# Last stage of a graph network kernel: edge slots summed into windows of 128 nodes that step by 64, in place of node tiles

## The chip, the cores and the metric

The kernel runs on one core of a Trainium2 chip. The metric is the device time of one execution in microseconds. The kernel before took 3025.7 us (median of 3 runs, 3021.4 to 3028.46).

## The reference, cut to what is computed

Four blocks follow each other, each added to x (6250 nodes of 256 features): a graph convolution over 100000 edges, a mixture of 8 experts, a second graph convolution, and a second mixture of 32 experts of which each node takes the one with the highest score. The change touches the second convolution and what follows it:

```python
h = layernorm(x) @ weight                                  # L1_gnn
msgs = edge_weight[:, None] * h[src]
x = x + segment_sum(msgs, dst, 6250) + bias
xf = layernorm(x)                                          # L1_ffn
idx = argmax(xf @ router_w.T + router_b)
x = x + relu(relu(xf @ W1[idx] + b1[idx]) @ W2[idx] + b2[idx])
```

The edges come sorted by `dst`, the node that an edge adds to. Both ends are drawn uniformly, so that 16 edges on average go to each node and 2048 to a tile of 128 nodes.

## The kernel before, in words

Nodes are held in 49 tiles of 128 rows. The edges are padded to 784 columns of 128 edges, and four columns (512 edges, 32 nodes on average) make a slot: 196 slots. Four programs run one after the other. The first converts the edge lists, checks them and computes the first products; the second does the first convolution and the 8 experts; a general path for edge lists that don't fit (`edge_block`) is skipped when the check of the first program finds nothing; the last stage, from line 1836, does the second convolution and the 32 experts.

In the last stage a loop over slots s is written out in full on each engine, with semaphores between them:

- GpSimd (POOL) issues four indirect DMAs per slot (line 2024). Each fetches 128 rows of 2 KB of `h_tab[1]`, one for each edge, into a ring of four slots (`got`). Slot s waits until the products of slot s - 4 are done (`s_prod`).
- VectorE (DVE) makes in its slot s the one-hot matrices of slot s + 1 (`one_hot`, line 2227): for each of the four columns a high and a low table, in which row e has the weight of edge e in the column of its node. There are two buffers, so that it waits for the products of slot s - 1.
- TensorE (PE) multiplies them with the fetched rows (`edges`, lines 2125 to 2127), three matmuls per column and node tile (high by high, high by low, low by high), and sums in one of two banks, `tile_bank(t)`. Slots 1 and 2 of a tile's four (s % 4) reach one node tile. Slots 0 and 3 lie at an edge of a tile and reach two, with a table 256 wide and 24 matmuls in place of 12. I call these wide and the others narrow slots.
- When a tile's last slot is done, DVE adds the bank to the tile's rows (line 2261), and takes the layer norm's statistics. Over the next six slots the tile is normalised, transposed and routed to its expert (lines 2188, 2197, 2203 on PE; 2267 to 2307 on DVE).
- The expert layers run from slot 11 on, for groups of four tiles: one step of the 16 per group in each slot. A step is 7 matmuls of 512 columns (`hidden`, lines 2142 to 2146), a ReLU on ScalarE (ACT, line 2076), its low half on DVE (line 2254), and 12 matmuls of 256 columns (`outputs`, lines 2163 to 2167) two slots later. After the 196th slot 26 more remain, with expert work alone.
- SyncE (SP) loads a group's rows from `acc_tab` (line 2045) after the rows of three groups before have been stored (line 2060), since they share the place.

The order of the work in a slot on PE is `edges(s)`, `outputs`, `hidden`, then a tile's small steps. On DVE it is the four additions of a finished group (line 2245), `one_hot(s + 1)`, the low half, then the tile's steps. In the first program `outside()` counts the edges that lie outside the reach of their slot's tiles (lines 743 to 756).

Of the kernel before, what the change touches and what calls it, by code (L numbers as in the profile page):

```python
# [61 lines left out]
FARS = 7  # L62
# [18 lines left out]
def build(nc, x, src, dst, wgt, wl, wr, bl, br, gw, gbr, w1, b1, g1, be1, m1, v1,  # L81
          w2, b2, g2, be2, m2, v2, wo, bo, lw, lb, rw, rb, mw1, mb1r, mw2, mb2, out):
    ctx = ExitStack()
    with ctx:
# [138 lines left out]
        with ExitStack() as c1:  # L223
# [53 lines left out]
            with ExitStack() as cc, nc.Block() as block:  # L277
# [58 lines left out]
                def _(pool):  # L336
# [35 lines left out]
                                   base=0, channel_multiplier=0).then_inc(s_const, 1)  # L372
                    nc.gpsimd.memset(ones[:, :], 1.0).then_inc(s_const, 1)
# [270 lines left out]
                def _(dve):  # L644
                    dve.wait_ge(s_const, 11)
# [9 lines left out]
                    nc.vector.tensor_copy(rel_n[:, :], node_i[:, :]).then_inc(s_bsum, 1)  # L655
# [85 lines left out]
                    def outside():  # L741
# [4 lines left out]
                        nc.vector.tensor_scalar(same[:, :], rel_n[:, :], float(2 * P), None, ALU.is_ge).then_inc(s_far, 1)  # L746
# [3 lines left out]
                        dve.wait_ge(s_far, 3)  # L750

                        def between(a):
                            return a[:, :].rearrange("p (t j) -> p t j", t=NTILES)[:, :, REACH:-REACH]
# [1082 lines left out]
        with ExitStack() as c4, nc.Block() as block:  # L1836
# [91 lines left out]
            hot_h = sb4("n1_hot_h", [P, 2, U, 2 * P], F32R)  # L1928
            hot_l = sb4("n1_hot_l", [P, 2, U, 2 * P], F32R)
# [46 lines left out]
            def node_tiles(s):  # L1976

                t, r = divmod(s, U)
                pairs = ((t - 1, 0), (t, P)) if r == 0 else ((t, 0), (t + 1, P)) if r == U - 1 else ((t, 0),)
                return [(q, at) for q, at in pairs if 0 <= q < NTILES]  # L1980

            def tile_bank(t):
                return bank[6 + t % 2][:, 0:D]
# [21 lines left out]
            def _(pool):  # L2005
                nc.gpsimd.iota(iota_i[:, :], pattern=[[1, 2 * P]], base=0, channel_multiplier=0).then_inc(s_node, 1)

                first = node_i[:, :].rearrange("p (t j) -> p t j", t=NTILES)
                nc.gpsimd.iota(first[:, :, 0:REACH], pattern=[[P, NTILES], [0, REACH]], base=-P,
                               channel_multiplier=0).then_inc(s_node, 1)  # L2010
                nc.gpsimd.iota(first[:, :, REACH:], pattern=[[P, NTILES], [0, EDGE_TILES // NTILES - REACH]],
                               base=0, channel_multiplier=0).then_inc(s_node, 1)
# [51 lines left out]
            def _(act):  # L2064
                act.wait_ge(s_keep, 1)
                act.wait_ge(s_node, 5)
# [43 lines left out]
            def _(pe):  # L2110
                def edges(s):
                    for t, at in node_tiles(s):

                        if t >= 2 and s == t * U - 1:
                            pe.wait_ge(s_sum, t - 1)

                    pe.wait_ge(s_got[s % RING], (s // RING + 1) * (16 * U))
                    pe.wait_ge(s_hot, s + 1)
                    for u in range(U):
                        for t, at in node_tiles(s):  # L2120
                            begins = u == 0 and s == max(t * U - 1, 0)
                            ends = u == U - 1 and s + 1 == edges_end(t)
                            w_h, w_l = hot_h[:, s % 2, u, at:at + P], hot_l[:, s % 2, u, at:at + P]
                            m_h, m_l = (got[:, s % RING, u, a:a + D] for a in (0, D))
                            nc.tensor.matmul(tile_bank(t), w_h, m_h, start=begins, stop=False)  # L2125
                            nc.tensor.matmul(tile_bank(t), w_h, m_l, start=False, stop=False)  # L2126
                            last = nc.tensor.matmul(tile_bank(t), w_l, m_h, start=False, stop=ends)  # L2127
                    last.then_inc(s_prod, 1)
# [77 lines left out]
            def _(dve):  # L2206
                nc.vector.tensor_copy(gidx, src_f[:, :]).then_inc(s_gidx, 1)
                nc.vector.tensor_scalar(wgt_f[:, :], wgt_f[:, :], keep[:, 0:1], None, ALU.mult).then_inc(s_keep, 1)
                dve.wait_ge(s_node, 3)
                nc.vector.tensor_copy(iota_f[:, :], iota_i[:, :]).then_inc(s_node, 1)  # L2210
                nc.vector.tensor_tensor(rel_n[:, :], dst_f[:, :], node_i[:, :], ALU.subtract).then_inc(s_node, 1)
                dve.wait_ge(s_node, 5)
# [6 lines left out]
                def one_hot(s):  # L2219

                    n = 2 * P if s % U in (0, U - 1) else P
                    if s >= 2:
                        dve.wait_ge(s_prod, s - 1)
                    for weight, table in ((dst_f, hot_h), (wgt_f, hot_l)):
                        for u in range(U):
                            c = s * U + u
                            last = nc.vector.tensor_scalar(table[:, s % 2, u, 0:n], iota_f[:, 0:n], rel_n[:, c:c + 1],  # L2227
                                                           weight[:, c:c + 1], ALU.is_equal, ALU.mult)
# [9 lines left out]
                for s in range(SLOTS):  # L2238
# [145 lines left out]
```

## Time and profile before

| | |
|---|---|
| Median of 3 runs | 3025.7 us (3021.4 to 3028.46) |
| Span of the profiled execution | 3226.6 us |
| Instructions in the profile | 53400 |
| Last stage in the profile | 1891 to 3226 us, 1335 us |

The profile is of one execution, which was slower than the timed runs by 200.9 us. Nothing in it says where these went. Engines are named PE (matmul), PEld (its weight load), DVE, ACT, POOL and SP; a matmul's duration is modelled and overlaps the next one, so that the distance between two starts tells more than the duration. PEclk is the clock that was granted to TensorE as a share of 2.4 GHz. In the view by lines a group shows its count, its busy time and the mean of one, then the idle time of the engine before them and what ended it. "issue" is time for which the profile shows no cause.

### The profile page before, as it was taken

Reading aid. Unit: us, or ns where it says so; the run is one execution under the profiler, and the core shown is the slowest. Engines: PE = TensorE matmul, PEld = TensorE weight load, DVE = VectorE, ACT = ScalarE, POOL = GpSimd, SP = SyncE. Lnnn points to the kernel's source line nnn. Section 1 sums busy time; section 2 is a strip of 40 time slices with the busy share of each in tenths; the row PEclk is TensorE's granted clock in tenths of the full one; section 3 lists DMA queues with packets and bytes.
Section 4 is the critical chain, followed back from the end, with each engine's and each line's share of the span. In section 5 each row is a group of like instructions: output and inputs, shape, how many; then the busy total and the mean of one; then the engine's idle time right before and its main releaser. Section 6 shows DMA issues by size and latency. Waiting matters only on the chain. (4 is left out here: it accounts for less than half of the span.)

```text
span 3226.6 us, 53400 instructions
## 1 busy us (share of the span) xinstructions
PE 2795.6 (87%) x18900; PEld 2527.3 (78%) x18900; DVE 2177.2 (67%) x5025; ACT 1527.1 (47%) x3161; POOL 1939.5 (60%) x1692
## 2 busy tenths in 40 slices
PE   5899737899999999999999936799999998999999
PEld 5798626788888788888888736788888888888888
DVE  8889654667777777777776555566666666666653
ACT  4477456878888788888876510011111111111111
POOL 0455477677677677777772047666666666666640
PEclk9999856899999999999999977899999999999999
DMA  2143452223323332333231057767777676766650
GB/s 68 7 91 76 106 173 88 77 89 105 95 88 107 102 101 81 107 105 101 81 104 52 20 173 188 180 170 180 179 185 180 167 182 174 179 171 176 177 138 14
DMA packets 241570, 390.22 MB, mean 121 GB/s; under 512 B 43258, under 2 KB 114834, under 8 KB 241042
## 3 DMA queue, kind: packets, MB, share of 16 engines
q0 software_dynamic: 163072, 310.24, 37.3%
q1 hardware_dynamic: 77940, 74.90, 7.3%
q8 instruction: 153, 2.51, 0.3%
q10 hardware_dynamic: 288, 1.61, 0.1%
q14 instruction: 117, 0.96, 0.1%
HBM read 343.43 MB, written 43.19 MB: 120 GB/s over the span
## 5 line engine op out<-in xcount | busy, mean ns | idle before, releaser
L1328 POOL DMA_INDIRECT f_got<-h_tab,list_cols x784 | 964.5, 1230 | 348.9 <-issue 237.9
L2024 POOL DMA_INDIRECT n_got<-h_tab,edge_cols x784 | 802.2, 1023 | 429.6 <-issue 219.0
L2076 ACT ACTIVATE n_hrh<-bank 128x512 fp32r<-128x512 f32 (+1 forms) x208 | 119.3, 573 | 1080.7 <-remote 644.6
L1623 DVE TENSOR_TENSOR f_hlo<-edge_cols,f_hhi 128x1024 fp32r<-128x1024 f32 (+1 forms) x208 | 242.3, 1165 | 310.0 <-ACT f_hhi L1418 229.4
L1507 PE MATMUL bank<-f_mhi,f_hot 128*128 128x256 f32 x1168 | 326.2, 310 | 108.7 <-DVE f_mlo L1617 101.7
L2125 PE MATMUL bank<-n_got,n_hot_h 128*128 128x256 f32 x1168 | 355.0, 304 | 74.3 <-issue 47.5
L1388 ACT ACTIVATE f_got<-f_got,list_cols 128x256 f32<-128x256 f32 x784 | 333.7, 497 | 110.3 <-DMA f_got<-h_tab,list_cols 106.3
L1413 ACT ACTIVATE edge_cols<-bank,f_shf,f_scl 128x512 f32<-128x512 f32 (+1 forms) x416 | 296.4, 745 | 186.9 <-PE bank L1319 120.2
L2127 PE MATMUL bank<-n_got,n_hot_l 128*128 128x256 f32 x1168 | 341.6, 292 | 12.0 <-issue 11.5
L2126 PE MATMUL bank<-n_got,n_hot_h 128*128 128x256 f32 x1168 | 341.6, 293 | 9.9 <-issue 9.6
L2227 DVE TENSOR_SCALAR n_hot_h<-list_cols,rel_f,edge_cols 128x256 fp32r<-128x256 f32 (+1 forms) x784 | 250.5, 387 | 138.6 <-DMA acc<-acc_tab 93.4
L2254 DVE SCALAR_TENSOR_TENSOR n_hrl<-bank,n_hrh 128x512 fp32r<-128x512 f32 (+1 forms) x208 | 136.5, 656 | 306.0 <-ACT n_hrh L2076 209.5
L1507 PEld LDWEIGHTS bank<-f_mhi,f_hot 128*128 128x128 f32 x1168 | 244.3, 209 | 124.1 <-issue 118.7
L1508 PE MATMUL bank<-f_mlo,f_hot 128*128 128x256 f32 x1168 | 316.1, 302 | 0.4 <-issue 0.4
L2125 PEld LDWEIGHTS bank<-n_got,n_hot_h 128*128 128x128 f32 x1168 | 234.0, 200 | 88.8 <-issue 61.2
L380 POOL DMA_INDIRECT list<-runs,off_i x98 | 162.9, 1663 | 216.7 <-DVE off_i L739 101.8
L1617 DVE TENSOR_TENSOR f_mlo<-f_got,f_mhi 128x1024 fp32r<-128x1024 f32 x196 | 239.2, 1220 | 18.4 <-issue 12.3
L1508 PEld LDWEIGHTS bank<-f_mlo,f_hot 128*128 128x128 f32 x1168 | 245.4, 210 | 5.0 <-issue 0.9
L2227 DVE TENSOR_SCALAR n_hot_l<-list_cols,rel_f,edge_cols 128x256 fp32r<-128x256 f32 (+1 forms) x784 | 248.0, 395 | 0.0
L2126 PEld LDWEIGHTS bank<-n_got,n_hot_h 128*128 128x128 f32 x1168 | 234.5, 201 | 15.9 <-issue 14.1
L2127 PEld LDWEIGHTS bank<-n_got,n_hot_l 128*128 128x128 f32 x1168 | 234.0, 200 | 13.6 <-issue 13.4
L2165 PE MATMUL bank<-n_w2l,n_hrh 128*128 128x256 f32 x784 | 226.4, 289 | 15.0 <-issue 14.9
(332 smaller groups left out, 7462.7 us busy)
## 6 DMA issues: line engine op xcount, KB each, us to landing
f_got<-h_tab,list_cols POOLq DMA_INDIRECT x784
n_got<-h_tab,edge_cols POOLq DMA_INDIRECT x784
h_tab<-acc SPq DMA_DIRECT2D x37, 128.0 KB
edge_cols<-in_w SPq DMA_DIRECT2D x16, 256.0 KB
xn<-acc_tab SPq DMA_DIRECT2D x8, 512.0 KB
n_rows<-acc_tab SPq DMA_DIRECT2D x8, 512.0 KB
out_rows<-n_rows SPq DMA_DIRECT2D x8, 512.0 KB
acc<-in_x SPq DMA_DIRECT2D x4, 896.0 KB
```

What stands on the lines that cost most here:

```text
L1328: nc.gpsimd.indirect_dma_start(got[:, s % RING0, u, :], None, h_tab[0], bass.IndirectOffsetOnAxis(gidx0[:, s * U + u:s * U + u + 1], 0), b ...
L1388: last = nc.scalar.activation(got[:, s % RING0, u, :], got[:, s % RING0, u, :], ACT.Copy, scale=w0_f[:, c:c + 1])
L1413: nc.scalar.activation(rl[:, m, 0:w], bank[(i + m) % 3][:, 0:w], ACT.Relu, bias=shf[:, l, e, m:m + 1], scale=scl[:, l, e, m:m + 1]).then_i ...
L1507: nc.tensor.matmul(tile_bank(t), lhs, mhi[:, s % 2, u, :], start=begins, stop=False)
L1508: last = nc.tensor.matmul(tile_bank(t), lhs, mlo[:, s % 2, u, :], start=False, stop=ends)
L1617: nc.vector.tensor_tensor(mlo[:, s % 2, :, :], got[:, s % RING0, :, :], mhi[:, s % 2, :, :].bitcast(F32), ALU.subtract).then_inc(s_mlo, 1)
L1623: nc.vector.tensor_tensor(hlo[l][:, :, 0:w], rl[:, :, 0:w], hhi[l][:, :, 0:w].bitcast(F32), ALU.subtract).then_inc(s_lo[l], 1)
L2024: nc.gpsimd.indirect_dma_start(got[:, s % RING, u, :], None, h_tab[1], bass.IndirectOffsetOnAxis(gidx[:, s * U + u:s * U + u + 1], 0), bou ...
L2125: nc.tensor.matmul(tile_bank(t), w_h, m_h, start=begins, stop=False)
L2126: nc.tensor.matmul(tile_bank(t), w_h, m_l, start=False, stop=False)
L2127: last = nc.tensor.matmul(tile_bank(t), w_l, m_h, start=False, stop=ends)
L2227: last = nc.vector.tensor_scalar(table[:, s % 2, u, 0:n], iota_f[:, 0:n], rel_n[:, c:c + 1], weight[:, c:c + 1], ALU.is_equal, ALU.mult)
```

## The change

In place of node tiles, slots 2m - 1 and 2m are summed in one window m of 128 nodes, which begins at node 64 (m - 1). There are 99 windows. Each slot has tables 128 wide and 12 matmuls. A window lies in one bank, m % 2. It covers one node tile when m is odd, and the upper half of one tile and the lower half of the next when m is even, so that DVE adds it with one or two instructions (`window_parts`): 147 additions in place of 49. DVE adds window m in slot 2m + 1. The first half tile of tile t is added in slot 4t + 1, where before the tile was first touched in slot 4t + 5; the statistics stay in slot 4t + 5. In the first program the check of the edge lists follows the windows: three more iotas on POOL, two fewer instructions on DVE.

```diff
+WIN_TILES = 2 * U
+WINDOWS = (EDGE_TILES - 2 * U) // WIN_TILES + 2
+HALF_NODES = P // 2
...
+        def window_bases(cols, landed):
+            body = cols[:, U:EDGE_TILES - U].rearrange("p (m j) -> p m j", j=WIN_TILES)
+            nc.gpsimd.iota(cols[:, 0:U], pattern=[[0, U]], base=-HALF_NODES, channel_multiplier=0).then_inc(landed, 1)
+            nc.gpsimd.iota(body, pattern=[[HALF_NODES, WINDOWS - 2], [0, WIN_TILES]], base=0,
+                           channel_multiplier=0).then_inc(landed, 1)
+            nc.gpsimd.iota(cols[:, EDGE_TILES - U:], pattern=[[0, U]], base=(WINDOWS - 2) * HALF_NODES,
+                           channel_multiplier=0).then_inc(landed, 1)
...
+                    window_bases(rel_n[:, :].bitcast(I32), s_const)
...
-                    dve.wait_ge(s_const, 11)
+                    dve.wait_ge(s_const, 14)
...
-                        nc.vector.tensor_scalar(same[:, :], rel_n[:, :], float(2 * P), None, ALU.is_ge).then_inc(s_far, 1)
+                        nc.vector.tensor_scalar(same[:, :], rel_n[:, :], float(P), None, ALU.is_ge).then_inc(s_far, 1)
...
-                        nc.vector.tensor_scalar(between(same), between(rel_n), float(P), None, ALU.is_ge).then_inc(s_far, 1)
-                        dve.wait_ge(s_far, 4)
-                        nc.vector.tensor_reduce(far_n[:, 2:3], between(same), AX.XY, ALU.add).then_inc(s_far, 1)
...
+            def window_of(s):
+                return (s + 1) // 2
+            def window_bank(m):
+                return bank[6 + m % 2][:, 0:D]
+            def window_parts(m):
+                t, odd = divmod(m, 2)
+                parts = ((t, 0, P),) if odd else ((t - 1, HALF_NODES, P), (t, 0, HALF_NODES))
+                return [(q, a, b) for q, a, b in parts if 0 <= q < NTILES]
...
                 def edges(s):
-                    for t, at in node_tiles(s):
-                        if t >= 2 and s == t * U - 1:
-                            pe.wait_ge(s_sum, t - 1)
+                    m = window_of(s)
+                    opens, closes = s == 0 or s % 2 == 1, s % 2 == 0 or s == EGROUPS - 1
+                    if opens and m >= 2:
+                        pe.wait_ge(s_sum, m - 1)
...
                     for u in range(U):
-                        for t, at in node_tiles(s):
...
+                        w_h, w_l = hot_h[:, s % 2, u, :], hot_l[:, s % 2, u, :]
+                        nc.tensor.matmul(window_bank(m), w_h, m_h, start=(opens and u == 0), stop=False)
+                        nc.tensor.matmul(window_bank(m), w_h, m_l, start=False, stop=False)
+                        last = nc.tensor.matmul(window_bank(m), w_l, m_h, start=False, stop=(closes and u == U - 1))
...
                 def one_hot(s):
-                    n = 2 * P if s % U in (0, U - 1) else P
+                    at = P // 2 if window_of(s) % 2 == 0 else 0
...
+                    if s % 2 == 1 and s <= EGROUPS + 1:
+                        m = (s - 1) // 2
+                        dve.wait_ge(s_prod, min(s, EGROUPS))
+                        if m:
+                            dve.wait_ge(s_sum, m)
+                        for q, a, b in window_parts(m):
+                            dve.wait_ge(s_accin, group_of(q) * 16 + 16)
+                            last = nc.vector.tensor_tensor(row(q)[a:b, :], window_bank(m)[a:b, :], row(q)[a:b, :], ALU.add)
+                        last.then_inc(s_sum, 1)
                     t = tile_at(s, AT_SUM)
                     if t is not None:
-                        dve.wait_ge(s_prod, edges_end(t))
-                        dve.wait_ge(s_accin, group_of(t) * 16 + 16)
-                        nc.vector.tensor_tensor(row(t), tile_bank(t), row(t), ALU.add).then_inc(s_sum, 1)
-                        dve.wait_ge(s_sum, t + 1)
+                        dve.wait_ge(s_sum, 2 * t + 3)
                         nc.vector.bn_stats(stats[:, t % 2, :], row(t)).then_inc(s_stats, 1)
```

## Rows read from the trace of the kernel before

**Rows 1.** The page: busy times, and the granted clock in 40 slices.
```profile
PE 2795.6 (87%) x18900; PEld 2527.3 (78%) x18900; DVE 2177.2 (67%) x5025; ACT 1527.1 (47%) x3161; POOL 1939.5 (60%) x1692
PEclk9999856899999999999999977899999999999999
```
**Rows 2.** Windows: length, busy PE, PEld, DVE, ACT, POOL (instructions), clock, DMA share, GB/s.
```profile
1891.00:3226.00 1335.00, 1172.06 (x7753) 1064.19 (x7753) 814.71 (x2681) 169.03 (x411) 806.77 (x789) 0.94 0.65 168
...
1967.00:2100.00 133.00, 101.80 (x616) 94.74 (x616) 72.10 (x264) 11.07 (x39) 88.05 (x88) 0.78 0.70 179
2100.00:3100.00 1000.00, 915.77 (x6163) 828.77 (x6162) 633.07 (x2122) 126.34 (x314) 639.96 (x633) 0.97 0.69 176
3145.00:3220.00 75.00, 75.00 (x477) 67.22 (x475) 22.80 (x52) 15.85 (x31) 0.00 (x0) 1.00 0.02 8
```
**Rows 3.** Line 2024, the gathers: duration ns min/median/max, first and last start.
```profile
L2024 POOL DMA_INDIRECT n_got<-h_tab,edge_cols x784: 997/1003/3233, 1893.5 to 3126.4; - x196
```
**Rows 4.** Timeline of POOL: start, duration, what [idle before, releaser].
```profile
2419.22 1.00 POOL L2024 DMA_INDIRECT n_got<-h_tab,edge_cols  x1 [0.30 <-issue]
2422.47 1.13 POOL L2024 DMA_INDIRECT n_got<-h_tab,edge_cols  x1 [2.25 <-PE bank L2127]
```
**Rows 5.** Timeline of PE: first edge matmuls of slots, and a stall.
```profile
2408.93 0.36 PE L2125 MATMUL bank<-n_got,n_hot_h 128*128 128x256 f32 x1
...
2415.27 0.36 PE L2125 MATMUL bank<-n_got,n_hot_h 128*128 128x256 f32 x1
2415.47 0.28 PE L2126 MATMUL bank<-n_got,n_hot_h 128*128 128x256 f32 x1
2415.59 0.28 PE L2127 MATMUL bank<-n_got,n_hot_l 128*128 128x256 f32 x1
...
2419.80 0.28 PE L2125 MATMUL bank<-n_got,n_hot_h 128*128 128x256 f32 x1
...
2421.59 0.28 PE L2125 MATMUL bank<-n_got,n_hot_h 128*128 128x256 f32 x1 [0.91 <-issue]
...
2425.37 0.36 PE L2125 MATMUL bank<-n_got,n_hot_h 128*128 128x256 f32 x1
...
2431.48 0.36 PE L2125 MATMUL bank<-n_got,n_hot_h 128*128 128x256 f32 x1
```
**Rows 6.** Timeline of DVE: a narrow and a wide pair of tables, a tile's addition.
```profile
2440.12 1.12 DVE L2227 TENSOR_SCALAR n_hot_h<-list_cols,rel_f,edge_cols 128x128 fp32r<-128x128 f32 x4 [1.40 <-DMA acc<-acc_tab]
2441.15 1.11 DVE L2227 TENSOR_SCALAR n_hot_l<-list_cols,rel_f,edge_cols 128x128 fp32r<-128x128 f32 x4
2443.11 0.41 DVE L2261 TENSOR_TENSOR xn<-bank,xn 128x256 f32<-128x256 f32 x1
2443.56 0.43 DVE L2263 BATCH_NORM_STATS2 n_stats<-xn 128x6 f32<-128x256 f32 x1
2445.63 1.38 DVE L2227 TENSOR_SCALAR n_hot_h<-list_cols,rel_f,edge_cols 128x256 fp32r<-128x256 f32 x4
2446.92 1.38 DVE L2227 TENSOR_SCALAR n_hot_l<-list_cols,rel_f,edge_cols 128x256 fp32r<-128x256 f32 x4
```
**Rows 7.** Line 1699: a DVE instruction that reads a bank on 8 partitions.
```profile
L1699 DVE TENSOR_TENSOR f_gateT<-bank,f_gateT x13: 280/680/681, 511.6 to 1794.0; 8x512 fp32r<-8x512 f32 x12, 8x128 fp32r<-8x128 f32 x1
```
**Rows 8.** Timeline of SP and DVE: a group's store, its load, the first addition.
```profile
2389.25 0.38 SPq L2060 DMA_DIRECT2D out_rows<-n_rows  x1
2394.22 0.37 SPq L2045 DMA_DIRECT2D n_rows<-acc_tab  x1
...
2467.85 0.41 DVE L2261 TENSOR_TENSOR n_rows<-bank,n_rows 128x256 f32<-128x256 f32 x1
```
**Rows 9.** Timeline of the first program: an iota, DVE's wait, the check's last instruction.
```profile
4.93 0.77 POOL L371 IOTA node_i<- 128x588 int32 x1
13.11 0.63 DVE L667 CAST xnt<-base 112x896 f32<-112x896 int32 x1 [4.57 <-DMA hbuf<-in_wgt]
...
128.26 0.56 DVE L756 TENSOR_REDUCE far_n<-rel_f 128x1 f32<-128x392 f32 x1
```

More of the change, by code:

```diff
@@ L61 @@
 SCANS = 7
-FARS = 7
+FARS = 5
+WIN_TILES = 2 * U
+WINDOWS = (EDGE_TILES - 2 * U) // WIN_TILES + 2
+HALF_NODES = P // 2
 EARLY = 3
@@ L654, in _ @@
                     nc.vector.memset(lag[:, :], 0.0)
-                    nc.vector.tensor_copy(rel_n[:, :], node_i[:, :]).then_inc(s_bsum, 1)
+                    nc.vector.tensor_copy(rel_n[:, :], rel_n[:, :].bitcast(I32)).then_inc(s_bsum, 1)
                     dve.wait_ge(s_bsum, 1)
@@ L749, in outside @@
                                                        accum_out=far_n[:, 1:2]).then_inc(s_far, 1)
-                        dve.wait_ge(s_far, 3)
-                        def between(a):
-                            return a[:, :].rearrange("p (t j) -> p t j", t=NTILES)[:, :, REACH:-REACH]
-                        nc.vector.tensor_scalar(between(same), between(rel_n), float(P), None, ALU.is_ge).then_inc(s_far, 1)
-                        dve.wait_ge(s_far, 4)
-                        nc.vector.tensor_reduce(far_n[:, 2:3], between(same), AX.XY, ALU.add).then_inc(s_far, 1)
                     def scales(g):
@@ L1927, in build @@
             got = sb4("n1_got", [P, RING, U, 2 * D], F32R)
-            hot_h = sb4("n1_hot_h", [P, 2, U, 2 * P], F32R)
-            hot_l = sb4("n1_hot_l", [P, 2, U, 2 * P], F32R)
+            hot_h = sb4("n1_hot_h", [P, 2, U, P], F32R)
+            hot_l = sb4("n1_hot_l", [P, 2, U, P], F32R)
             wgt_h = dst_f.bitcast(F32R)
@@ L1974, in width @@
                 return WIDTHS[g]
[L1976 to L1983, printed above, removed]
+            def window_of(s):
[6 more added lines that the diff above has]
+                return [(q, a, b) for q, a, b in parts if 0 <= q < NTILES]
             def out_tile(k):
@@ L2005, in _ @@
             def _(pool):
[L2006 to L2012, printed above, removed]
+                nc.gpsimd.iota(iota_i[:, :], pattern=[[0, 2], [1, P]], base=0, channel_multiplier=0).then_inc(s_node, 1)
+                window_bases(node_i[:, :], s_node)
                 pool.wait_ge(s_gidx, 1)
@@ L2065, in _ @@
                 act.wait_ge(s_keep, 1)
-                act.wait_ge(s_node, 5)
+                act.wait_ge(s_node, 6)
                 nc.scalar.activation(wgt_h[:, :], wgt_f[:, :], ACT.Copy).then_inc(s_wgt, 1)
@@ L2119, in edges @@
                     for u in range(U):
-                        for t, at in node_tiles(s):
[L2121 to L2127, printed above, removed]
+                        w_h, w_l = hot_h[:, s % 2, u, :], hot_l[:, s % 2, u, :]
+                        m_h, m_l = (got[:, s % RING, u, a:a + D] for a in (0, D))
+                        nc.tensor.matmul(window_bank(m), w_h, m_h, start=(opens and u == 0), stop=False)
+                        nc.tensor.matmul(window_bank(m), w_h, m_l, start=False, stop=False)
+                        last = nc.tensor.matmul(window_bank(m), w_l, m_h, start=False, stop=(closes and u == U - 1))
                     last.then_inc(s_prod, 1)
@@ L2208, in _ @@
                 nc.vector.tensor_scalar(wgt_f[:, :], wgt_f[:, :], keep[:, 0:1], None, ALU.mult).then_inc(s_keep, 1)
-                dve.wait_ge(s_node, 3)
+                dve.wait_ge(s_node, 4)
                 nc.vector.tensor_copy(iota_f[:, :], iota_i[:, :]).then_inc(s_node, 1)
                 nc.vector.tensor_tensor(rel_n[:, :], dst_f[:, :], node_i[:, :], ALU.subtract).then_inc(s_node, 1)
-                dve.wait_ge(s_node, 5)
+                dve.wait_ge(s_node, 6)
                 dve.wait_ge(s_wgt, 1)
@@ L2226, in one_hot @@
                             c = s * U + u
-                            last = nc.vector.tensor_scalar(table[:, s % 2, u, 0:n], iota_f[:, 0:n], rel_n[:, c:c + 1],
+                            last = nc.vector.tensor_scalar(table[:, s % 2, u, :], iota_f[:, at:at + P], rel_n[:, c:c + 1],
                                                            weight[:, c:c + 1], ALU.is_equal, ALU.mult)
```

## The prediction

> **What bounds the kernel now.** I read the page first. PE is busy in 87% of the span and POOL in 60% [rows 1], but these are shares over four programs, and the change lies in the last. So the windows come next. The last stage takes 1335 us, and in its steady part, 2100 to 3100 us, PE is busy 915.8 of 1000 us, DVE 633.1, POOL 640.0 with 633 gathers, at a clock of 0.97 [rows 2]. Then the gathers' own line. The median is 1003 ns, and the first starts at 1893.5, the last at 3126.4 us [rows 3]. That is 1232.9 us for 783 intervals, 6.30 us per slot of four. The timeline of POOL shows what lies between: 0.30 us where it waits for nobody, which makes 1.307 us per gather, and 2.25 us where it waited for the edge matmuls, since the ring was full [rows 4]. At 1.307 us all 783 intervals would take 1023 us, 5.23 us per slot. So POOL is held back by 210 us, and PE holds it.
>
> PE's own pace stands in its timeline. From the first edge matmul of a slot to that of the next, undisturbed slots take 6.34 and 6.11 us (wide; starts 2408.93 to 2415.27 and 2425.37 to 2431.48) and 4.53 us (narrow; 2415.27 to 2419.80) [rows 5]. Two of each give 21.51 us, 5.38 us per slot. The remaining 0.92 us per slot are stalls and falls of the clock, such as the 0.91 us ahead of a matmul in the middle of a slot, for which the profile shows no cause [rows 5]. PE's idle time of 84 us in 1000 [rows 2] is the part of it that shows as idle. Once the gathers are done, at 8 GB/s, PE runs 75.00 of 75.00 us at clock 1.00 [rows 2]: the stalls go with the gathers' traffic.
>
> **The matmuls.** 98 slots are wide; the first and the last of the stage reach one tile only, so 96 lose 12 matmuls each, 1152 with their weight loads. Two neighbours start 0.12 us apart [rows 5], so 1.44 us per wide slot, 138 us in all. This is on the path. PE's undisturbed slots become 4.90, 4.67, 4.53 and 4.53, 4.66 us on average. Of some 38 matmuls per slot 32 remain; I let the stalls shrink with them, by a factor of 0.84.
>
> **The new limit.** 4.66 us is below POOL's 5.23. The gain ends where POOL no longer waits, so it is not 138 us but what of the 210 us is really there.
>
> **Profiled and timed.** The profiled span is 200.9 us above the median of 3025.7, and the profile doesn't show where these lie. If they are spread by length, the last stage has 200.9 x 1335 / 3226.6 = 83 us of them. If they lie in PE's stalls here, it can have at most 0.92 x 196 = 180 us, since PE can't be faster than undisturbed. I take 120 us. More than 83, because uncaused stalls are dense just here; well below 180, because that would leave no stall at all, and the clock of 0.97 alone costs 3% of 5.38 us, 0.16 us per slot or 31 us. So in a timed run the gathers take 1232.9 - 120 = 1113 us, 5.68 us per slot.
>
> **After, in a timed run.** PE: 4.66 + 0.84 x (0.92 - 0.61) = 4.92 us per slot. POOL: 5.23, so POOL binds. Its gathers take 1023 us, and 15 us for its other work and slow gathers: POOL's busy time of 806.8 us in the stage is 20 above 784 x 1.003 [rows 2, 3], and I leave a quarter of it as hidden. 1113 - 1038 = 75 us saved. PE now trails POOL by a full ring. The last gather starts 100 us before the end of the span [rows 3]. Slot 195 and the 26 slots of expert work behind it (4.53 - 1.44 = 3.09 us each) take 85 of these, which leaves 15 us by which PE trails. With the ring no longer full I take 8 us of them as gained. Two engines of nearly the same pace lose something to each other, and a group's first slot has 8 more matmuls on PE; I take 6 us. Sum 75 + 8 - 6 = 77 us, 3025.7 - 77 = 2949 us. Does POOL's 1.307 us hold in a timed run? Bounds: as it is, or scaled by 3025.7 / 3226.6 to 1.226, 960 us in all, where PE at 4.92 us (964 us) would take over. I keep 1.307, since gathers that wait for nothing agree within 10 ns. The other end is in the range.
>
> **DVE.** Its 98 wide tables fall from 1.29 to 1.03 us per four [rows 6], so 0.52 us per slot, -51 us in all. It gains 98 additions. Half of a tile is 64 partitions. The row of 8 partitions by 512 elements takes 0.68 us and the full tile's addition of 256 elements 0.41, 0.45 to the next start [rows 6, 7]: fewer partitions save nothing. So 98 x 0.45 = +44 us (lower bound, if half the height were half the price: 22). The sum is about -7 us, beside other work: DVE has 3.99 us of work per slot now, 76% of 5.23. The new waits: the addition of window m waits for the products of slot 2m, which `one_hot(s + 1)` ahead of it waits for already, and for DVE's own last addition. Queued behind them on DVE are the statistics, the expert choice and the next tables, for which PE waits. PE's wait for a bank comes every second slot in place of every fourth; the addition it needs is made two slots ahead of it, about 10 us. Both cost nothing while that cover holds.
>
> **Rows a tile earlier.** The first half of a tile is added four slots earlier, so a group's rows must be there sooner. A load was issued at 2394.22, 5.0 us after the store, and the first addition to it was at 2467.85 [rows 8]. 74 us less four slots of 5.23 leaves 53 us. A load would have to take ten times the 5.0 us of a store to matter: 0. If it did, DVE would stand still with PE's tables behind it. SP's queue keeps its order.
>
> **The first program.** Three iotas, of 776 and twice 4 columns, by the 0.77 us of one of 588 [rows 9], take at most 1.3 us. They hold DVE's start, but DVE then waits 4.57 us for a load [rows 9]: 0; without that cover 1.3 us. Two instructions of at most 0.56 us go [rows 9]: -1 to 0 us, in noise. That the check may send everything to the general path is excluded by the inputs: from the reference's own draw the smallest and the largest offset of an edge in its window are 27 and 114, inside 0 to 127.
>
> **The rivals.**
> - The stalls are the kernel's own. By length (83 us) a slot is 5.87 us before; POOL still binds after it: 1150 - 1038 + 8 = 120 us, 2906. With none of the 200.9 us in this stage PE stays the bound at 4.66 + 0.84 x 0.92 = 5.43 us, the gain is 0.87 x 196 = 170 us, 2856. For it: a full ring, and stalls only beside the gathers' traffic, which a timed run has too. Against it: the missing 201 us must lie somewhere. 0.20.
> - PE is nearly undisturbed already. With all 180 us here a slot takes 5.38 us before, POOL's limit is just below, and 1053 - 1038 + 8 = 23 us are left, 3003. For it: 0.15 us between the two paces. Against it: it needs a timed run without any stall. 0.15.
> - DVE in slots 4t + 1. Tables 2.06, low half 0.6, two additions 0.9, statistics 0.9, expert choice 1.2: 5.7 us, over 5.23. If the two table buffers don't even this out, 49 x 0.47 = 23 us go, 2972. 0.08.
> - Slower: the clock. From 1967 to 2100 us PE was busy 77% of the time and the granted clock was 0.78 on average, between the levels of 1.2 and 2.4 GHz, against 0.97 at 92% [rows 2]. After the change PE has gaps in every slot. At 0.78 a slot takes 4.66 / 0.78 + 0.26 = 6.23 us, 0.55 us over 5.68, +108 us, 3134. It decides where the clock falls below 0.86 over the stage. Against it: 4.92 of 5.23 us is still 94% busy, more than in the steady part now. 0.04. The Trainium skill ("TensorE: Matmul & The Clock Gate", the sections on the HAM clock gate and its oscillation) says that the clock is halved by default, that activity releases it and that waits for DMA let it fall back; by that rule, feeding PE from POOL's pace would be where this case begins. The trace agrees in its rows of 0.78.
>
> **How the numbers follow.** Forecast 2949 with its own range of 2920 to 2975: 0.50; 0.03 is for what I don't see. The range from 2885 to 3003 takes in the forecast, DVE's case, POOL's shorter gather and most of the first two rivals; 0.17 is left out. A measurement of this kernel can tell about 0.2%, 6 us. Faster 0.92, same 0.03, slower 0.05.
>
> **What would show it.** In the profile after: 784 gathers as now, most after 0.30 us; POOL's waits for the edge matmuls almost gone; 2352 edge matmuls; every undisturbed slot of 4.5 to 4.9 us; DVE's 147 additions of 0.41 us at either height; clock over 0.9 from 2100 us on; the profiled gain larger than the timed one, 100 to 190 us. It is wrong if gathers still wait for products in most slots, if their spacing itself has changed, or if the clock is below 0.86.

## The result, and the profile after

The changed kernel takes 2993.3 us (median of 4 runs, 2985.1 to 2997.5), the kernel before beside it 3025.3 us. The ratio is 0.9899 (95% interval 0.9877 to 0.9922), a gain of 32 us where 77 were forecast. Executions of the kernel before come at about 3025 us or, some of them and whole sets of runs too, at about 3200 to 3230 us; the page behind [rows 1] is of the second kind, all timed runs shown ahead of the prediction are of the first, and every ratio below compares a kernel with the kernel before in its own set.

The page of the changed kernel: busy times, the granted clock in 40 slices, and the chain that ended last, by engine.

```profile
PE 2614.2 (87%) x17748; PEld 2360.3 (79%) x17748; DVE 2166.4 (72%) x5121; ACT 1523.2 (51%) x3161; POOL 1932.4 (65%) x1696
PEclk9999966799999999999999997689999999999999
...
POOL 16%; issue 15%; PE 6%; DMA 1%; POOLq 1%; DVE 0%; DVEq 0%
```

1152 matmuls are gone (18900 in [rows 1], 17748 here), and the chain lies on POOL: on its gathers and on "issue", time of POOL for which the profile shows no cause, such as the 0.30 us between two gathers. The windows of the changed kernel, columns as in [rows 2]: the last stage, its opening, and 800 us of its steady part.

```profile
1862.00:2990.00 1128.00, 996.63 (x6601) 895.43 (x6601) 802.16 (x2777) 167.08 (x411) 801.04 (x786) 0.95 0.78 198
1930.00:2060.00 130.00, 101.20 (x622) 93.87 (x623) 88.68 (x339) 13.89 (x47) 99.80 (x100) 0.82 0.83 208
2000.00:2800.00 800.00, 742.49 (x5003) 664.50 (x5004) 598.88 (x2125) 118.91 (x302) 614.32 (x610) 0.99 0.84 213
```

The gathers' own line, 2030 in the changed kernel, answers to [rows 3].

```profile
L2030 POOL DMA_INDIRECT n_got<-h_tab,edge_cols x784: 999/1003/3251, 1861.6 to 2900.6; - x196
its engine sat idle before it (us, times) until:
  issue: 234.9, 771
  PE bank L2129: 3.7, 12
```

First to last gather is 1039.0 us; 1038 were forecast. POOL waits for the products 3.7 us in all. The timeline of POOL, which answers to [rows 4], shows one gather every 1.31 us with nothing but 0.30 us between:

```profile
2399.99 1.00 POOL L2030 DMA_INDIRECT n_got<-h_tab,edge_cols  x1 [0.31 <-issue]
2401.30 1.01 POOL L2030 DMA_INDIRECT n_got<-h_tab,edge_cols  x1 [0.30 <-issue]
2402.61 1.07 POOL L2030 DMA_INDIRECT n_got<-h_tab,edge_cols  x1 [0.30 <-issue]
2403.98 1.00 POOL L2030 DMA_INDIRECT n_got<-h_tab,edge_cols  x1 [0.30 <-issue]
```

The timeline of PE, first edge matmuls of four slots (line 2127), answers to [rows 5]. Now PE waits for the rows:

```profile
2399.97 0.36 PE L2127 MATMUL bank<-n_got,n_hot_h 128*128 128x256 f32 x1 [0.46 <-issue]
...
2405.63 0.39 PE L2127 MATMUL bank<-n_got,n_hot_h 128*128 128x256 f32 x1 [0.75 <-DMA n_got<-h_tab,edge_cols]
...
2410.56 0.36 PE L2127 MATMUL bank<-n_got,n_hot_h 128*128 128x256 f32 x1
...
2415.68 0.39 PE L2127 MATMUL bank<-n_got,n_hot_h 128*128 128x256 f32 x1 [0.42 <-DMA n_got<-h_tab,edge_cols]
```

So the state after is the forecast one: POOL sets the pace at 1.307 us per gather. What was wrong is the state before, and the first experiment shows it.

### The profile page after: what moved, and what is told of

Read it like the earlier page. It is cut to its first block and busy times, and to the rows that moved or that the text cites. A ratio compares the mean times of both kernels' runs of the same rounds, so it can differ in the third digit from the quotient of the medians.

```text
span 2989.7 us, 51246 instructions
## 1 busy us (share of the span) xinstructions
PE 2614.2 (87%) x17748; PEld 2360.3 (79%) x17748; DVE 2166.4 (72%) x5121; ACT 1523.2 (51%) x3161; POOL 1932.4 (65%) x1696
## 5 line engine op out<-in xcount | busy, mean ns | idle before, releaser
L2127 PE MATMUL bank<-n_got,n_hot_h 128*128 128x256 f32 x784 | 246.8, 315 | 138.5 <-DMA n_got<-h_tab,edge_cols 62.3
L2127 PEld LDWEIGHTS bank<-n_got,n_hot_h 128*128 128x128 f32 x784 | 156.6, 200 | 183.0 <-issue 85.4
L393 POOL DMA_INDIRECT list<-runs,off_i x98 | 156.3, 1594 | 223.7 <-DVE off_i L752 99.4
L2229 DVE TENSOR_SCALAR n_hot_h<-list_cols,rel_f,edge_cols 128x128 fp32r<-128x128 f32 x784 | 224.2, 366 | 74.1 <-PE bank L2129 73.7
L1323 PE MATMUL bank<-f_whi,f_hhi 128*128 128x256 f32 x784 | 225.6, 288 | 6.0 <-DVE f_hlo L1629 6.0
L2129 PE MATMUL bank<-n_got,n_hot_l 128*128 128x256 f32 x784 | 230.0, 293 | 0.0
L2128 PE MATMUL bank<-n_got,n_hot_h 128*128 128x256 f32 x784 | 229.9, 293 | 0.0
L1324 PE MATMUL bank<-f_wlo,f_hhi 128*128 128x256 f32 x784 | 224.1, 286 | 0.0
L1325 PE MATMUL bank<-f_whi,f_hlo 128*128 128x256 f32 x784 | 223.9, 286 | 0.0
L2229 DVE TENSOR_SCALAR n_hot_l<-list_cols,rel_f,edge_cols 128x128 fp32r<-128x128 f32 x784 | 223.7, 369 | 0.0
```

The lines of the kernel that those rows point to most:

```text
L2127: nc.tensor.matmul(window_bank(m), w_h, m_h, start=(opens and u == 0), stop=False)
L2128: nc.tensor.matmul(window_bank(m), w_h, m_l, start=False, stop=False)
L2129: last = nc.tensor.matmul(window_bank(m), w_l, m_h, start=False, stop=(closes and u == U - 1))
L2229: last = nc.vector.tensor_scalar(table[:, s % 2, u, :], iota_f[:, at:at + P], rel_n[:, c:c + 1], weight[:, c:c + 1], ALU.is_equal, ALU.mult)
```

## The experiments

They ran in six sets, each with the kernel before beside it. Each ratio has its 95% interval.

### The kernel before once more (e1_before_again)

No edit. What does the last stage look like in an execution whose length agrees with the timed runs?

> The kernel before, profiled a second time. Theory 1 (PE was nearly undisturbed in the timed runs, and the 201 us by which the first profile exceeded them lay mostly in the last stage): span near 3023 us, last stage near 1160 us, gathers spaced so that a slot takes 5.40 us instead of 6.30, PE's uncaused stalls gone. Theory 2 (the stalls are the kernel's own, and the change lost its gain elsewhere, on DVE or by the clock): slots of 5.7 to 5.9 us in the last stage, and the stalls still there.

3024.4 us, ratio 1.0 (0.9985 to 1.0014); the profiled span is 3025.7 us. Its windows (columns as above), and the gathers' own line:

```profile
1862.00:3024.00 1162.00, 1098.73 (x7753) 1027.27 (x7753) 816.42 (x2681) 166.96 (x411) 802.53 (x789) 0.97 0.76 193
1930.00:2060.00 130.00, 105.15 (x731) 99.02 (x732) 88.44 (x317) 13.32 (x46) 100.12 (x99) 0.90 0.83 208
2000.00:2800.00 800.00, 793.42 (x5706) 743.23 (x5705) 586.78 (x1968) 115.06 (x294) 598.72 (x595) 1.00 0.82 207
```

```profile
L2024 POOL DMA_INDIRECT n_got<-h_tab,edge_cols x784: 997/1003/3245, 1864.4 to 2926.9; - x196
its engine sat idle before it (us, times) until:
  issue: 234.7, 735
  PE bank L2127: 28.6, 49
```

The timeline of PE, first edge matmuls of five slots:

```profile
2401.57 0.36 PE L2125 MATMUL bank<-n_got,n_hot_h 128*128 128x256 f32 x1
...
2407.91 0.36 PE L2125 MATMUL bank<-n_got,n_hot_h 128*128 128x256 f32 x1
...
2412.44 0.28 PE L2125 MATMUL bank<-n_got,n_hot_h 128*128 128x256 f32 x1
...
2416.92 0.36 PE L2125 MATMUL bank<-n_got,n_hot_h 128*128 128x256 f32 x1
...
2423.03 0.37 PE L2125 MATMUL bank<-n_got,n_hot_h 128*128 128x256 f32 x1
```

The distances are 6.34, 4.53, 4.48 and 6.11 us, the same as the undisturbed slots of [rows 5], but here every slot is like that: PE is busy 793 of 800 us at clock 1.00. First to last gather is 1062.5 us, against 1232.9 in [rows 3]. So of the 200.9 us by which the page exceeded the median, 170.4 lay between the first and the last gather, 29.1 ahead of the stage (first gather 1893.5, here 1864.4) and 1.4 behind. PE was the bound with almost no stall, at 5.44 us per slot (worked out in the next experiment), and POOL's 5.23 lay right below it.

### One gather of four left out, in both kernels (e2_before_3g, e3_after_3g)

If POOL is taken away as a bound, what do the matmuls alone give? The fourth column of edges is multiplied with the third column's rows, so a quarter of the rows is left out and the number of matmuls stays.

```diff
-                    for u in range(U):
+                    for u in range(U - 1):
...
-                    pe.wait_ge(s_got[s % RING], (s // RING + 1) * (16 * U))
+                    pe.wait_ge(s_got[s % RING], (s // RING + 1) * (16 * (U - 1)))
...
-                            m_h, m_l = (got[:, s % RING, u, a:a + D] for a in (0, D))
+                            m_h, m_l = (got[:, s % RING, min(u, U - 2), a:a + D] for a in (0, D))
```

> The kernel before with three gathers per slot instead of four in the last stage; the fourth column of edges uses the third's rows, so a quarter of the gathered rows is left out. POOL's own pace falls from 5.23 to 3.92 us per slot. Theory 1: PE is the bound at 5.38 us, so the time hardly moves, 3010 to 3027 us. If POOL or the traffic had been a part of the bound before: under 3000.

> The changed kernel with three gathers per slot instead of four in the last stage; the fourth column of edges uses the third's rows. Theory 1: POOL was the bound, now PE is, at 4.66 to 4.9 us per slot: (5.31 - 4.8) x 196 = 100 us less than the changed kernel, 2893 (2870 to 2920). Theory 2 (DVE's additions or the clock hold the changed kernel): over 2960.

The kernel before with three gathers: 2987.6 us, ratio 0.9886 (0.9861 to 0.991), more of a gain than expected. The changed kernel with three: 2867.3 us, 0.949 (0.9465 to 0.9514); once more (e14_after_3g_again, below) 2866.3. Between the two lie 120 us, where the matmuls removed are worth 138. Windows of the kernel before with three gathers: everything in the steady part, then line 2125 alone, opening and steady part (columns: PE, PEld, clock, DMA share, GB/s).

```profile
2000.00:2800.00 800.00, 800.00 (x5763) 750.05 (x5762) 583.59 (x1977) 116.37 (x294) 447.26 (x442) 1.00 0.63 158
...
1862.00:2000.00 138.00, 56.95 (x179) 38.32 (x179) 0.87 0.84 221
2000.00:2800.00 800.00, 258.35 (x882) 168.17 (x881) 1.00 0.63 158
```

Line 2125 alone in the kernel before (e1):

```profile
1862.00:2000.00 138.00, 46.93 (x132) 32.41 (x132) 0.76 0.83 219
2000.00:2800.00 800.00, 259.15 (x882) 168.63 (x881) 1.00 0.82 207
```

Line 2125 has 6 matmuls per slot on average (8 and 4). The steady part has 882 with four gathers and with three, 147 slots of 5.44 us: there POOL costs the kernel before nothing. In the opening it has 132 against 179, about 22 slots against 30, and 8 slots of 5.44 us are the 43 us by which the spans differ (some 6 of them go with a start that is earlier here, 1858.8 us). So for most of its first 22 slots the kernel before was bound by POOL already. It is POOL's own pace and not the traffic: POOL runs 101 instructions in these 138 us with four gathers per slot (e1, 219 GB/s), 100 with three (e2, 221 GB/s) and 99 with rows of half the size (e5 below, 121 GB/s). This explains the miss in e2. It also explains, by the same count of 99 in e3, why the removed matmuls are worth 120 and not 138: in the opening POOL sets the pace with three gathers too.

The changed kernel with three gathers, everything and then line 2127 alone (4 matmuls per slot):

```profile
2000.00:2700.00 700.00, 700.00 (x4920) 649.43 (x4918) 577.88 (x2071) 117.41 (x296) 452.17 (x447) 1.00 0.73 182
...
2000.00:2700.00 700.00, 175.91 (x593) 112.41 (x592) 1.00 0.73 182
```

593 / 4 = 148 slots in 700 us, 4.72 us per slot, PE never idle. From 5.44 this is 0.72 us less, half of the 1.44 us that was worked out for a wide slot. With four gathers the changed kernel runs at 5.26 (608 matmuls of line 2127 in 800 us, 152 slots). Of the 0.72 us per slot, POOL lets 0.18 through.

### The removed matmuls put back (e4_after_24mm)

In the changed kernel the wide slots get 24 matmuls again; tables, windows and additions stay new.

```diff
                         nc.tensor.matmul(window_bank(m), w_h, m_l, start=False, stop=False)
+                        if s % U in (0, U - 1):
+                            for right in (m_h, m_l, m_h):
+                                nc.tensor.matmul(window_bank(m), w_h, right, start=False, stop=False)
```

> The changed kernel with the 12 matmuls put back into each of the 98 slots that had 24: the first product of each column is summed three more times, partly with other halves, so the sums are not the reference's. Theory 1: PE's pace is again 5.38 us per slot and the time that of the kernel before, 3025 (3015 to 3035). Theory 2: above it by what DVE's additions cost, 3040 or more.

3026.7 us, ratio 1.0011 (0.9999 to 1.0022). The window and the wait:

```profile
2000.00:2800.00 800.00, 792.83 (x5698) 743.54 (x5699) 573.26 (x2041) 115.02 (x292) 598.49 (x595) 1.00 0.82 207
```

```profile
  PE bank L2132: 33.2, 54
```

PE is busy 793 of 800 us again and POOL waits 33.2 us for products, as 28.6 in e1. The whole gain is the matmuls'. The rest of the change (half-height additions, narrower tables, three iotas) makes no difference that can be measured; by the interval it costs 7 us at most. Slots 0 and 195 had 12 matmuls in the kernel before and have 24 here, so the page counts 18924 matmuls in place of 18900. At 0.12 us each that is an estimated 3 us, about the 2.2 us between the two medians.

### Half the bytes per gather (e5_after_1kb, e13_after_1kb_again)

What sets the 1.307 us, POOL's issuing or the traffic? Each gather fetches rows of 1 KB in place of 2 KB.

```diff
-                            got[:, s % RING, u, :], None, h_tab[1],
+                            got[:, s % RING, u, 0:D], None, h_tab[0],
...
-                        m_h, m_l = (got[:, s % RING, u, a:a + D] for a in (0, D))
+                        m_h, m_l = (got[:, s % RING, u, a:a + D] for a in (0, 0))
```

> The changed kernel, with gathered rows of 1 KB instead of 2 KB in the last stage: they are read from the first table, and the low halves of the messages are left out (their high halves are used twice), at the same number of matmuls and of gathers. Theory 1a (POOL's issue of 1.307 us per gather is the bound): the time stays at 2993 within 8 us, and the gathers stay 1.31 us apart. Theory 1b (the DMA engines, 84% busy at 213 GB/s, are the bound): traffic halves, and the time falls towards PE's pace, up to 100 us.

2994.7 us, ratio 0.9905 (0.9888 to 0.9922), no different from the changed kernel.

```profile
2000.00:2800.00 800.00, 743.37 (x5005) 665.72 (x5006) 600.86 (x2128) 119.30 (x303) 614.35 (x610) 0.99 0.50 114
```

The DMA share falls from 0.84 to 0.50 and the rate from 213 to 114 GB/s, and still 610 instructions run on POOL in 800 us. Half the traffic changes nothing, so what binds is POOL's issuing, and the next experiment changes that alone. The repeat in another set:

> The changed kernel with gathered rows of 1 KB (low halves of the messages left out) a second time. With the kernel before at 3025 us: 2995 as before. With it at 3200 us, where PE's uncaused stalls make a slot 6.1 us: if the stalls come from the gathers' traffic, half of it brings the time towards 2995; if they come with the number of gathers or with neither, 3167 stays.

2990.1 us, 0.9902 (0.9884 to 0.9919).

### The gathers without their bounds check (e6_after_nobound)

```diff
-                            bass.IndirectOffsetOnAxis(gidx[:, s * U + u:s * U + u + 1], 0),
-                            bounds_check=ROWS - 1, oob_is_err=True).then_inc(s_got[s % RING], 16)
+                            bass.IndirectOffsetOnAxis(gidx[:, s * U + u:s * U + u + 1], 0)).then_inc(s_got[s % RING], 16)
```

> The changed kernel without the bounds check of the indices in the last stage's gathers; one register instruction less on POOL for each. Theory 1a: the time follows POOL's distance between two gathers, 784 times. If the bound check costs nothing on POOL the distance stays 1.31 us and the time 2993; if the 0.30 us between two gathers hold work for it and shrink to 0.25, the time falls by 39 us, to 2954.

2949.8 us, ratio 0.976 (0.974 to 0.978): the fastest version that computes all of the reference, 45 us below e5 and e7, which ran in the same set at the changed kernel's pace (2994.7 and 2994.8). It drops a safeguard: an index outside the table would no longer be reported. The gathers' line, its timeline, and the window:

```profile
L2030 POOL DMA_INDIRECT n_got<-h_tab,edge_cols x784: 936/938/3248, 1860.3 to 2853.6; - x196
```

```profile
2401.47 0.94 POOL L2030 DMA_INDIRECT n_got<-h_tab,edge_cols  x1 [0.30 <-issue]
```

```profile
2000.00:2800.00 800.00, 771.29 (x5264) 698.74 (x5265) 625.83 (x2234) 125.11 (x317) 605.09 (x640) 0.99 0.86 223
```

The gather itself shrinks from 1003 to 938 ns, and the 0.30 us between two stays. First to last gather falls from 1039.0 to 993.3 us, 46 us, and the time by as much: POOL's pace is the kernel's pace. By the 0.065 us alone it would be 51 us; POOL now waits 9.1 us for products, where it waited 3.7. That the total meets the 2949 of the forecast is chance.

### Twice the additions (e7_after_quarters)

Is DVE near the limit? Every addition is split into quarters of a tile, 392 in place of 147.

```diff
-                return [(q, a, b) for q, a, b in parts if 0 <= q < NTILES]
+                return [(q, c, c + P // 4) for q, a, b in parts if 0 <= q < NTILES for c in range(a, b, P // 4)]
```

> The changed kernel, each window added in pieces of 32 partitions: 392 additions of 256 elements instead of 147, the same result. Theory 1 (DVE has cover): 245 x 0.45 = 110 us more of DVE's work leave the time at 2993, within 8 us, since DVE's work per slot rises from some 3.9 to 4.5 us and stays below POOL's 5.23. Theory 2 (DVE's additions were what took the gain): up to 110 us slower.

2994.8 us, ratio 0.9904 (0.9888 to 0.9921).

```profile
2000.00:2800.00 800.00, 740.64 (x4995) 662.47 (x4994) 680.91 (x2312) 119.59 (x304) 614.69 (x609) 0.99 0.84 213
```

DVE works 681 of 800 us in place of 599, and the time doesn't move.

### The sets at 3200 us

The question was whether POOL's gathers cost the kernel before anything: the bounds check is taken from the last stage of the kernel before (before_nobound), and from both convolutions of the changed one (after_nobound2). The edit is that of e6, in the second case at the first convolution's gathers (line 1335) as well. In these three sets the kernel before itself took 3200.5, 3196.2 and 3230.4 us.

> The kernel before without the bounds check in the last stage's gathers. With the change the same edit gave 44 us, 0.058 us for each of the 784 gathers. Theory 1: here PE is the bound at 5.47 us per slot, so POOL's faster 5.00 us brings only what it brings in the first 11 to 20 slots, before the expert work fills PE: 20 x 0.23 = 5 us, 3020 (3012 to 3026). If POOL had been the bound before the change: 45 us, 2980.

> The changed kernel without the bounds check in the gathers of the last stage and of the second program. In the second program PE is busy 91% and POOL waits for the low halves of the messages, so 784 shorter gathers should bring little: 2950 as with the last stage alone, down to 2940 if its gathers also touch the path.

> The kernel before without the bounds check in the last stage's gathers, a second time, since all kernels of the runs e8 and e9 were slower by 175 us, the kernel before among them. If the kernel before takes 3025 us here: PE is its bound, so 3012 to 3026 us, a ratio over 0.995. If the kernel before takes 3200 us again, PE's uncaused stalls of the first profile are there, and the ratio is that of e8, 0.997.

> The changed kernel without the bounds check in the gathers of the last stage and the second program, a second time. With the kernel before at 3025 us: 2950, down to 2940. With it at 3200 us: 3179 again.

> The changed kernel as it is. With the kernel before at 3025 us: 2993, POOL's distance of 1.31 us between two gathers as the bound. With it at 3200 us: if PE's matmuls count under such stalls, my forecast for stalls that are the kernel's own, 120 to 170 us less, 3030 to 3080; if something else sets the pace of a slot then, little, over 3160.

> The kernel before without the bounds check in the last stage's gathers, with the kernel before at 3025 us. Theory 1: PE is its bound at 5.47 us per slot, and POOL's shorter gathers bring only 5 us of the first slots and a few short waits, 3020 (3012 to 3026). If POOL is the bound in it too: 45 us less, 2980.

> The changed kernel without the bounds check in both places, with the kernel before at 3025 us: 2950 as without it in the last stage alone, down to 2940.

| run | us | ratio to the kernel before (95%) |
|---|---|---|
| e8_before_nobound | 3193.0 | 0.9973 (0.9954 to 0.9992) |
| e9_after_nobound2 | 3179.0 | 0.9922 (0.9893 to 0.9951) |
| e10_before_nobound | 3190.1 | 0.9994 (0.9974 to 1.0014) |
| e11_after_nobound2 | 3173.1 | 0.9915 (0.9881 to 0.995) |
| e12_after_again, the changed kernel | 3166.8 | 0.9913 (0.9889 to 0.9938) |
| e15_before_nobound | 3232.9 | 0.9996 (0.9967 to 1.0025) |
| e16_after_nobound2 | 3226.8 | 0.9974 (0.9946 to 1.0002) |

The question stays unanswered by them, since something else sets the pace here. e2 answers it for the runs at 3025 us: POOL costs the kernel before something in the opening, and only there. after_nobound2 was never timed in a set at 3025 us. What the profile shows of the other pace, in the changed kernel (e12): the window, then a stretch of PE's timeline.

```profile
2000.00:2800.00 800.00, 694.79 (x4253) 616.62 (x4253) 511.23 (x1836) 102.01 (x263) 528.99 (x524) 0.90 0.73 182
```

```profile
2406.08 0.28 PE L2129 MATMUL bank<-n_got,n_hot_l 128*128 128x256 f32 x1 [0.53 <-issue]
2406.20 0.29 PE L2127 MATMUL bank<-n_got,n_hot_h 128*128 128x256 f32 x1
2407.52 0.28 PE L2128 MATMUL bank<-n_got,n_hot_h 128*128 128x256 f32 x1 [1.04 <-issue]
2408.24 0.28 PE L2129 MATMUL bank<-n_got,n_hot_l 128*128 128x256 f32 x1 [0.44 <-issue]
...
2413.06 0.63 PE L2145 MATMUL bank<-n_xnl,n_w1h 128*128 128x512 f32 x1
2413.48 0.63 PE L2146 MATMUL bank<-n_xnh,n_w1l 128*128 128x512 f32 x1
```

524 gathers in 800 us make 131 slots of 6.11 us, though PE alone needs 4.72 and POOL 5.23. PE stands still in the middle of a slot, 1.04 us between two matmuls on the same rows and the same table among others, and behind these stalls two matmuls of 512 columns lie 0.42 us apart, at 1.2 GHz, where they lie 0.23 us apart in the first page of the changed kernel (2402.89 and 2403.12 us). Such stalls are those of [rows 5]. The kernel before without the bounds check has 519 gathers in the same 800 us (e8), 6.17 us per slot.

The traces show one thing more that sets these executions apart. In the page before, POOL's wait of 2.25 us in [rows 4] is for the products of the slot that starts at 2415.27 us in [rows 5]. The first line here is the last matmul of that slot, the second is DVE, which waits for the same products:

```profile
2416.66 0.28 PE L2127 MATMUL bank<-n_got,n_hot_l 128*128 128x256 f32 x1
...
2421.67 1.38 DVE L2227 TENSOR_SCALAR n_hot_h<-list_cols,rel_f,edge_cols 128x256 fp32r<-128x256 f32 x4 [1.98 <-DMA acc<-acc_tab]
```

By its start and duration the matmul ends at 2416.94, but DVE goes on at 2421.67 and POOL at 2422.47, 5.5 us later, just after PE's own stall ends at 2421.59. In between PE has started 25 later matmuls. In e1 the same three lines lie close together:

```profile
2404.39 0.28 PE L2127 MATMUL bank<-n_got,n_hot_l 128*128 128x256 f32 x1
2404.72 1.11 DVE L2227 TENSOR_SCALAR n_hot_h<-list_cols,rel_f,edge_cols 128x128 fp32r<-128x128 f32 x4 [1.44 <-PE bank L2127]
2405.52 1.00 POOL L2024 DMA_INDIRECT n_got<-h_tab,edge_cols  x1 [1.20 <-PE bank L2127]
```

The page before has 106 such waits of POOL of over 0.4 us, 218 us in all. In 78 of them, 171 us, POOL goes on more than 2 us after the end of the last matmul that it waits for. The page puts 155 us of these waits down to `acc<-acc_tab`, a transfer of the general path, which does not run here:

```profile
  DMA acc<-acc_tab: 155.4, 69
```

The other seven traces of executions at 3165 to 3240 us have 73 to 85 such late waits each. The ten traces of the shorter kind have one each, and in e1 the distance is 0.84 us at 35 of 36 waits. So in the slower executions POOL and DVE wait for a signal of PE that comes long after the matmuls behind it have ended by the trace. Why the signal is late, and whether PE's stalls are its cause or its effect, is not shown.

The lower clock takes its part too. In e12 PE is idle 0.80 us per slot at a clock of 0.90, in e8 0.53 us at 0.97. So of the 0.72 us by which the change shortens PE's slot little is left. All four traces of changed kernels of this kind have 0.90 from 2000 to 2800 us, the four of kernels before 0.96 or 0.97.

No edit here brings this pace about or ends it: the set of e12 and, minutes later on the same chip, the set of e13 and e14 (kernel before 3022.6 us) differ by 174 us for the same kernel. So do the sets of e1 and e8 on another chip, by 176 us. e13 and e14 were to tell whether the stalls go with the gathers, but met the pace of 3025 us. The cause stays open. The changed kernel gains 0.9% at this pace too (e12), but hardly through the limits worked out here, since neither is reached.

> The changed kernel with three gathers per slot (a quarter of the rows left out) a second time. With the kernel before at 3025 us: 2867. With it at 3200 us: if the stalls go with the traffic or with the gathers, a quarter of them goes, 3167 - 0.25 x 1.48 x 196 = 3095 or less; if they come with PE's own instructions, 3167 stays.

2866.3 us, ratio 0.949 (0.9473 to 0.9506), a repeat of e3 in the set at 3022.6 us.

## Why the prediction was right or wrong

**The step that failed** is "Profiled and timed: I take 120 us". Of the 200.9 us above the median, 170 lay between the gathers and not 120. Both reasons for staying below 180 failed. The first was that "that would leave no stall at all", and there is almost none (e1, PE busy 793 of 800 us). The second was that "the clock of 0.97 alone costs 3% of 5.38 us", and the clock is 1.00 there: its loss came with the stalls. With 1062.5 us in place of 1113 the prediction's own sum gives 1062.5 - 1038 + 8 = 32.5 us (26.5 with its 6 us for two engines of nearly the same pace), and the measured gain is 32. This was the second rival (PE nearly undisturbed already, 3003 us, 0.15); its 23 us are short of 32 mainly because it took 5.38 us per slot where PE really needs 5.44. The rival that calls the stalls the kernel's own (0.20) is refuted: e1 hasn't got them.

One reading before the sum was wrong as well: "So POOL is held back by 210 us, and PE holds it.". In e1 the gathers take 39 us more than 1023, not 210. In the page that was read 171 us of POOL's waits end long after the matmuls that they are for. There a late signal held POOL, and that is no work which the change could remove.

**The matmuls** came out as worked out: 0.72 us per slot where PE binds (e2, e3; 4.72 us after, 4.66 forecast). The 138 us come to 120 between e2 and e3, because the opening is POOL's. The prediction priced the opening like the rest of the stage.

**The new limit** was right: 1039.0 us for the gathers by 1038. In profiles the gain is 1062.5 - 1039.0 = 23.5 us between the gathers, 9.7 us behind them (98.8 us from the last gather to the end in e1, 89.1 after; 8 were forecast), and 2.8 us of an earlier start, which is inside what starts scatter by (1851 to 1864 us over these profiles). The 6 us for two engines of nearly the same pace do not show. That 1.307 us would hold in a timed run was right as well, and e5 and e6 show what it is: POOL's own work, not traffic.

**DVE** cost nothing, as forecast. The changed kernel's additions, line 2266 by form, answer to the addition in [rows 6]:

```profile
L2266 DVE TENSOR_TENSOR n_rows<-bank,n_rows 64x256 f32<-64x256 f32 x66 | 27.8, 422 | 2.8 <-DMA n_rows<-acc_tab 1.3
L2266 DVE TENSOR_TENSOR n_rows<-bank,n_rows 128x256 f32<-128x256 f32 x33 | 13.7, 414 | 0.0
```

Half the height takes 422 ns and the full height 414. The Trainium skill ("VectorE: DVE Perf Modes", the section on why tensor_reduce can't reduce along the partition axis) calls each partition a lane with a pipeline of its own; the trace agrees. The rival in slots 4t + 1 (0.08) fell with e7. The rows needed a tile earlier were there: DVE waited for them once, 1.3 us, in the same row. The cover for PE's wait on an addition did fail four times, 10.5 us of PE in all and 9.1 of them before 2000 us, but PE had room there: POOL set the pace. The iotas of the first program don't show in e4.

**The clock** rival (0.04) was wrong for the runs at 3025 us: PE waits ahead of a slot's first edge matmul 95 times in 152 slots and is busy 742.5 of 800 us, and the clock is 0.99. Only in the opening is the clock lower than in the kernel before, 0.82 against 0.90 from 1930 to 2060 us, and the opening is POOL's in both kernels (98 and 96 gathers from 1862 to 2000 us). The rule of the Trainium skill ("TensorE: Matmul & The Clock Gate", the section on the clock's oscillation) that was named, that waits for DMA let the clock fall back, does not show in the steady part: the 45 waits for rows there are 0.64 us on average and 2.3 us at most, and the clock stays up. In the opening waits for rows last up to 7.1 us, and the clock is 0.68 from 1862 to 2000 us. At the pace of 3200 us the clock is lower in the changed kernels, 0.90 against 0.96 or 0.97, though not below the 0.86 of the rival.

**What would show it.** Right: 784 gathers, most after 0.30 us, 2352 edge matmuls, 147 additions of 0.41 us, the clock. Not to be told from the page: the undisturbed slots of 4.5 to 4.9 us, since PE waits in most slots; in e3, where it doesn't, the mean is 4.72. Wrong: the profiled gain, given as 100 to 190 us. From [rows 1] it is 237, since the two pages are of different paces; against e1 it is 36.

## What to carry to other kernels

Put the span of the page beside the timed median first; where they differ by more than the runs do among themselves, price nothing by the page's stalls, waits or clock but by the pace that each engine has where nothing disturbs it (here 5.44 us for PE and 5.23 for POOL, whose distance of 4% was all that could be had). A cut on the engine that binds is worth the distance to the next one: 138 us of matmuls gave 32, and the next 45 came from POOL. When a wait ends, look at when the instruction ended that it waits for: here 0.84 us before in one kind of execution, over 2 us before in most waits of the other. A stage can have an opening in which another engine binds, and a cut brings nothing there.

## What was not expected of the hardware

- The bounds check costs POOL 0.065 us in each indirect DMA of 128 rows (1003 ns with, 938 without, e6); with 784 gathers that bind, the kernel was 45 us faster without it, 1.5%.
- The gather's 1.0 us and the 0.30 us behind it didn't change with the size of a row: 2 KB and 1 KB rows give the same pace, at 213 and 114 GB/s (e5).
- The same kernel on the same chip took 3196 us in one set of runs and 3023 in the next, both sets being even in themselves. Of the 175 us between the two pages of the changed kernel 155 lie between the first and the last gather. The slower traces have stalls of PE without a cause in the trace, and POOL and DVE go on up to several us after the matmuls that they wait for have ended.
